# Running the compressed-KV projection of an MLA layer in half groups of 256 tokens, on 8 cores

## The chip, the cores and the metric

One Trainium2 chip, all 8 cores. Cores 0 to 3 take the first sequence of the batch, cores 4 to 7 the second. There is no exchange between cores. The metric is device microseconds of the slowest core for one execution of the whole program.

## The reference

One layer: `x + attention(LN(x)) + ffn(LN(x))` for x of 2 x 4096 x 4096. The part that matters here is the key/value side of the attention:

```python
xn = _layernorm(x, axis=-1)
ckv = hidden_states @ Wkv_a                       # 4096 -> 512 + 64
compressed, k_pe = (ckv[..., :KV_RANK], ckv[..., KV_RANK:])
kv = _rmsnorm(compressed, kv_a_ln_w) @ Wkv_b
...
k_pe = _apply_rope(k_pe, cos, sin)
```

The rest is the query side (rank 1536), causal softmax attention with 32 heads, the output projection, and a feed-forward part with a dense base matrix and 28 rank-8 adapters of which two are taken per token.

## The kernel before, in words

Each core computes the keys and values of its whole sequence (4096 tokens) and the queries of 8 tiles of 128 tokens. The program has four stages with barriers between them: stage 0 (LayerNorm of all tokens, transposition, `Wkv_a`, RMS norm, rope of the key part), stage 1 (the same for the own tiles with `Wq_a`), stage 2 (attention, head pair by head pair), stage 3 (output projection and feed-forward). The instructions of each engine are written in program order by a small helper, `Prog.do`, whose line 64 is the line that the profile names for all of them, so the rows are told apart by their tile names. Semaphores `p`, `v`, `a` count TensorE, VectorE and ScalarE; DMAs have rings of four (SyncE) and eight (GpSimd) semaphores.

Stage 0 is a loop over 8 groups `g` of 4 tiles of 128 tokens. For a tile `t`:

- GpSimd's queue loads `x_full` to `p0_x[t % 2]` with a cast to bf16, once the LayerNorm two tiles before has read the buffer.
- VectorE runs eight `bn_stats` (tile name `p_bn`), an aggregation and small operations, with two activations on ScalarE, and writes the normalised tile to `p0_xn[t % 2]`. It starts only when the transpose of tile `t - 2` has landed, because that reads the same buffer.
- SyncE issues one DMA transpose of 128 x 4096 from `p0_xn[t % 2]` into the columns of the tile in `p0_xnTg`, the transposed group (32 blocks of 128 features by 512 tokens). The first of a group also waits for the matmuls of the group before (`xnT_war`).

After the four tiles TensorE multiplies. For each of five chunks `mc` of the 576 output features (four of 128, one of 64) it runs 32 matmuls of 512 moving columns into one of three PSUM banks `ps_ck`; here a round is one such chunk. After each of the first four rounds VectorE copies the bank to `p0_cf`, squares it into the single buffer `p0_sq`, and TensorE adds the squares over the features by a matmul with a column of ones into `ps_ss`:

```python
ck_evac[mc % 3] = mark("v")
wait("tensor", "v", ck_evac[mc % 3])
...
do("tensor", "matmul", ps_ss[0:1, :], g_ones_col[:], sqs,
   start=(mc == 0), stop=(mc == 3), inc="p")
```

The next round stands behind that matmul on TensorE. The square of a chunk waits for the ones-column matmul of the chunk before. The tail of a group follows: the fifth chunk is copied (`p_kpef`), the mean of squares is taken (`p_ssr`), two activations give its inverse root, a matmul spreads it over the partitions (`ps_bc`), VectorE scales the four chunks into `g_cnorm`, and a rotation matmul and three operations of VectorE make the rope part `g_kpe`. On VectorE the next group's first LayerNorm stands behind all this in the queue.

Of the kernel before, what the change touches and what calls it, by code (L numbers as in the profile page):

```python
# [7 lines left out]
BF16 = mybir.dt.bfloat16  # L8
# [29 lines left out]
class Prog:  # L38
# [15 lines left out]
    def do(self, eng, meth, *args, inc=None, **kw):  # L54
        sem = amt = None
        r = None
        if inc is not None:
            key, amt = inc if isinstance(inc, tuple) else (inc, 1)
            self.cnt[key] += amt
            sem = self.sems[key]  # L60
            r = self.cnt[key]

        def f(e, meth=meth, args=args, kw=kw, sem=sem, amt=amt):
            ins = getattr(e, meth)(*args, **kw)  # L64
            if sem is not None:
                ins.then_inc(sem, amt)

        self.q[eng].append(f)
        return r
# [9 lines left out]
    def wait(self, eng, key, val):  # L79
        if val <= 0:  # L80
            return
        self.q[eng].append(lambda e, s=self.sems[key], v=val: e.wait_ge(s, v))
# [9 lines left out]
    def mark(self, key):  # L92
        return self.cnt[key]
# [9 lines left out]
def build_nc(debug=0, p0_groups=8, do_p0c=True, p0_stage=100, npairs=NPAIR):  # L103
# [58 lines left out]
    with es_root:  # L162
        P = Prog(nc, es_root)
        do, wait, mark = P.do, P.wait, P.mark

        def sb(name, shape, dt, stack):
            return stack.enter_context(nc.sbuf_tensor(name, shape, dt))

        def ps(name, stack, shape=None):
            return stack.enter_context(  # L170
                nc.psum_tensor(name, shape or [128, 512], F32))
# [11 lines left out]
        tok_con = [P.dma("gpsimd", dst[:], src) for dst, src in  # L183
                   [(g_ident, ident_in), (g_qlnw, qlnw), (g_kvlnw, kvlnw)]]
        do("gpsimd", "memset", g_ones_col[:], 1.0, inc="q")
        do("gpsimd", "memset", g_ones_row[:], 1.0, inc="q")
        c_consts_q = mark("q")

        es0 = ExitStack()
        with es0:  # L190
            x_sb = [sb(f"p0_x{i}", [128, D], BF16, es0) for i in range(2)]
            xn_sb = [sb(f"p0_xn{i}", [128, D], BF16, es0) for i in range(2)]
            xnT_g = sb("p0_xnTg", [128, 32 * 512], BF16, es0)
            wkva_sb = sb("p0_wkva", [128, 32 * 576], BF16, es0)

            rk_sb = sb("p0_rk", [64, 64], BF16, es0)
# [13 lines left out]
            rsr = sb("p0_rsr", [1, 512], F32, es0)  # L210
            rbc = sb("p0_rbc", [128, 512], F32, es0)

            ps_ck = [ps(f"ps_ck{i}", es0) for i in range(3)]
            ps_ss = ps("ps_ss", es0)
            ps_bc = ps("ps_bc", es0)
            ps_rk = ps("ps_rk", es0)
# [1 line left out]
            tok_p0 = [  # L218
                P.dma("gpsimd",
                      wkva_sb[:].rearrange("p (k f) -> p k f", k=32),  # L220
                      wkv_a.rearrange("(k p) f -> p k f", p=128)),
                P.dma("gpsimd", rk_sb[:], rk_in),
            ]
# [30 lines left out]
                return mark("v")  # L254

            tr_marks = [None, None]
            ck_evac = [0, 0, 0]
            xnT_war = 0
            prev_rope_v = 0
            prev_ssr_v = 0  # L260
            prev_kpe_a = 0
            prev_prk = 0
            for g in range(p0_groups):
                for tt in range(4):
                    t = g * 4 + tt
                    par = t % 2
                    if t >= 2:
                        wait("gpsimd", "v", ln_state[par])
                    gl = P.dma("gpsimd", x_sb[par][:],
                               x_full[t * 128:(t + 1) * 128, :])  # L270
                    P.wait_t("vector", gl)
                    P.wait_t("vector", tr_marks[par])
                    ln_state[par] = emit_ln(par)
                    if p0_stage < 2:
                        continue
                    wait("sync", "v", ln_state[par])
                    if tt == 0:
                        wait("sync", "p", xnT_war)
                    tr_marks[par] = P.dma(
                        "sync",  # L280
                        xnT_g[:].rearrange("p (k f) -> p k f", f=512)[:, :, tt * 128:(tt + 1) * 128],
                        xn_sb[par][:].rearrange("p (k f) -> p k f", f=128),
                        meth="dma_start_transpose")
                if p0_stage < 3:
                    continue
                P.wait_t("tensor", tr_marks[0])
                P.wait_t("tensor", tr_marks[1])
                if g == 0:
                    for tk in tok_p0 + tok_con:
                        P.wait_t("tensor", tk)  # L290
                    wait("tensor", "q", c_consts_q)
                wait("tensor", "a", prev_kpe_a)
                xnT3 = xnT_g[:].rearrange("p (k f) -> p k f", f=512)
                wk3 = wkva_sb[:].rearrange("p (k f) -> p k f", f=576)
                ssmm = [0, 0]
                first_ss = True
                for mc in range(5 if p0_stage >= 40 else 4):
                    pb = ps_ck[mc % 3]
                    wait("tensor", "v", ck_evac[mc % 3])
                    lo = mc * 128  # L300
                    hi = min(lo + 128, 576)
                    for kc in range(32):
                        do("tensor", "matmul",
                           pb[0:hi - lo, :], wk3[:, kc, lo:hi], xnT3[:, kc, :],
                           start=(kc == 0), stop=(kc == 31),
                           inc=("p" if kc == 31 else None))
                    pm = mark("p")
                    if mc < 4:
                        sqs = sq_f32[:]
                        wait("vector", "p", pm)  # L310
                        do("vector", "tensor_copy",
                           c_f32[:, mc * 512:(mc + 1) * 512], pb[:], inc="v")
                        cv = mark("v")
                        wait("vector", "v", cv)
                        wait("vector", "p", ssmm[0])
                        do("vector", "tensor_mul", sqs,
                           c_f32[:, mc * 512:(mc + 1) * 512],
                           c_f32[:, mc * 512:(mc + 1) * 512], inc="v")
                        ck_evac[mc % 3] = mark("v")
                        wait("tensor", "v", ck_evac[mc % 3])  # L320
                        if first_ss:
                            wait("tensor", "v", prev_ssr_v)
                            first_ss = False
                        do("tensor", "matmul", ps_ss[0:1, :], g_ones_col[:], sqs,
                           start=(mc == 0), stop=(mc == 3), inc="p")
                        ssmm[0] = mark("p")
                    else:
                        wait("vector", "p", pm)
                        do("vector", "tensor_copy", kpe_f[:], pb[0:64, :], inc="v")
                        kv_m = mark("v")  # L330
                        wait("scalar", "v", kv_m)
                        wait("scalar", "p", prev_prk)
                        do("scalar", "activation", kpe_bf[:], kpe_f[:], AF.Copy, inc="a")
                        ck_evac[mc % 3] = mark("v")
                kpe_vm, kpe_am = mark("v"), mark("a")
                pss = ssmm[0]
                if p0_stage < 4:
# [14 lines left out]
                   start=True, stop=True, inc="p")  # L352
# [11 lines left out]
                if p0_stage < 42:  # L364
# [5 lines left out]
                   start=True, stop=True, inc="p")  # L370
# [21 lines left out]
                prev_kpe_a = kpe_am  # L392
                if debug >= 1 and g == 7:
# [2 lines left out]
                    P.dma("gpsimd", dbg["d_misc"][:, 512:1024], kt1[:])  # L396
                    P.dma("gpsimd", dbg["d_misc"][:, 1024:1536], kt2[:])
                    P.dma("gpsimd", dbg["d_misc"][:, 1536:2048], cosf[:])
                xnT_war = mark("p")

            p0b_v, p0b_a = mark("v"), mark("a")

# [15 lines left out]
        with es1:  # L418
# [16 lines left out]
            tr_marks = [None, None]  # L435
            ln2 = {}
            for t in range(8):
# [7 lines left out]
                for i in range(8):  # L445
# [3 lines left out]
                       inc=("v" if i == 7 else None))  # L449
# [5 lines left out]
                   LN_EPS, inc="v")  # L455
# [39 lines left out]
            for mc in range(12):  # L495
# [10 lines left out]
                for half in range(2):  # L506
                    pb = ps_q[half]
                    wait("tensor", "v", qevac[half])
                    for kc in range(32):
                        do("tensor", "matmul", pb[:],  # L510
                           wq3[par][:, kc, :], xo3[:, kc, half * 512:(half + 1) * 512],
                           start=(kc == 0), stop=(kc == 31),
                           inc=("p" if kc == 31 else None))
                    pm = mark("p")
# [13 lines left out]
                       start=(mc == 0), stop=(mc == 11), inc="p")  # L528
# [17 lines left out]
               start=True, stop=True)  # L546
            do("tensor", "matmul", ps_qb[1][:], g_ones_row[:], qrsr[0:1, 512:1024],
               start=True, stop=True, inc="p")
# [17 lines left out]
        if debug != 1:  # L566
# [30 lines left out]
            for dst, src in [(cosq_sb, cosq), (sinq_sb, sinq),  # L597
                             (masks_sb, masks), (rq_sb, rq_in)]:
                tk = P.dma("gpsimd", dst[:], src)
# [126 lines left out]
            if True:  # L726
# [89 lines left out]
                for p in range(npairs):  # L816
                    for stp in range(NSLOT):
                        for h01 in ((0, 1) if p % 2 == 0 else (1, 0)):
# [4 lines left out]
                                p=p, h01=h01, s=s, stp=stp, nk5=nk5,  # L823
# [36 lines left out]
        else:  # L860
# [34 lines left out]
            for kc in range(32):  # L895
# [4 lines left out]
                for tch in range(8):  # L900
                    do("tensor", "matmul", ps_l[:, tch * 28:(tch + 1) * 28],
                       xk[par][:, tch * 128:(tch + 1) * 128], gw3[:, kc, :],
                       start=(kc == 0 and tch == 0), stop=(kc == 31),
                       skip_group_check=True)
                for er in range(2):
                    for half in range(2):
# [3 lines left out]
                           start=(kc == 0), stop=(kc == 31),  # L910
                           skip_group_check=True,
                           inc=("p" if (er == 1 and half == 1) else None))
# [6 lines left out]
            for tch in range(8):  # L919
                lo = lg_sb[:, tch * 28:(tch + 1) * 28]  # L920
# [33 lines left out]
                   inc="p")  # L954
# [14 lines left out]
            for er in range(2):  # L969
                for half in range(2):  # L970
                    if er == 1:
# [4 lines left out]
                       start=True, stop=True, inc="p")  # L976
# [44 lines left out]
            for dc in range(8):  # L1021
# [7 lines left out]
                for kc in range(32):  # L1029
# [8 lines left out]
                    for qc in range(8):  # L1038
                        if kc == 0:
# [3 lines left out]
                           start=(kc == 0), stop=False)  # L1043
# [160 lines left out]
```

How the kernel before makes its waits and increments, by code:

```python
        def f(e, meth=meth, args=args, kw=kw, sem=sem, amt=amt):  # L63
            ins = getattr(e, meth)(*args, **kw)
            if sem is not None:
                ins.then_inc(sem, amt)
# [12 lines left out]
    def wait(self, eng, key, val):  # L79
        if val <= 0:
            return
        self.q[eng].append(lambda e, s=self.sems[key], v=val: e.wait_ge(s, v))
```

## Time and profile before

| | us |
|---|---|
| median of 2 timed runs | 6434.42 (6394.51 and 6474.34) |
| profiled execution, its own time | 6153.71 |
| its span, slowest core | 6151.8 |
| stage 0, to the end of the last group | 0 to about 1199 |
| stage 1 | about 1199 to 1650 |
| stage 2 | about 1650 to 4820 |
| stage 3 | about 4820 to 6152 |

Busy time over the span: TensorE 3819.0 us (62%), VectorE 1887.9 (31%), ScalarE 1696.6 (28%), GpSimd 444.9 (7%). The chain of waits that ended last is 54% TensorE and 20% DMA; the DMA transposes of stage 0 alone are 7% of the span in it. A page of the profile gives for each group of instructions the busy time, the mean duration and the idle time ahead of it with the releaser; the rows behind this section come from such views.

### The profile page before, as it was taken

To read this page: it belongs to the slowest core of one execution; us is meant where nothing else is said; L and a number is where in the kernel's file an instruction comes from. 1 tells how busy PE (TensorE), PEld (TensorE's weight loads), DVE (VectorE), ACT (ScalarE), POOL (GpSimd) and SP (SyncE) were. 2 spreads that over 40 slices of the span, in tenths; PEclk is the share of its full clock that TensorE was granted. 3 is DMA by queue.
4 is the path that set the end of the run, shared out by engine and by line. 5 is a ranking of instruction groups with operands and counts; after the bars stand their busy time and mean duration, and the time that the engine had idled before them with its cause. 6 is when DMAs were issued, how large, how long until landed. Compare 5 with 4: busy or idle time off the path is not lost.

```text
span 6151.8 us, 55137 instructions; the slowest of 8 cores (6115.0 to 6151.8 us)
## 1 busy us (share of the span) xinstructions
PE 3819.0 (62%) x17980; PEld 1749.3 (28%) x17980; DVE 1887.9 (31%) x2827; ACT 1696.6 (28%) x1812; POOL 444.9 (7%) x773
## 2 busy tenths in 40 slices
PE   0233332208567776777667777677777538888887
PEld 0111111103233333333233333333333213333333
DVE  1222223321244444444444444444444010000000
ACT  0000000000054455544565455554555100000000
POOL 0000000000000000000000000000000112222222
PEclk9667666659877766777667776777767569999998
DMA  9755555595333323333243332333232465555555
GB/s 101 56 57 57 56 57 57 68 149 52 53 58 58 60 52 69 61 61 61 48 74 60 62 60 52 69 60 61 53 64 57 86 159 89 89 89 89 87 86 93
DMA packets 960482, 434.94 MB, mean 71 GB/s; under 512 B 832978, under 2 KB 935392, under 8 KB 954608
## 3 DMA queue, kind: packets, MB, share of 16 engines
q0 software_dynamic: 197072, 238.45, 23.3%
q1 hardware_dynamic: 763136, 192.98, 21.8%
q8 instruction: 155, 2.54, 0.2%
q14 instruction: 119, 0.97, 0.1%
HBM read 362.92 MB, written 34.08 MB: 65 GB/s over the span
## 4 chain that ended last, share of the span: by engine, by line
PE 54%; DMA 20%; issue 8%; DVE 8%; ACT 7%; SPq 2%; another core or an unknown queue 0%; POOL 0%; DVEq 0%; ACTq 0%; POOLq 0%
PE ps_b L64 30%; PE ps_acc L64 15%; DMA p_xnTg<-p_xn 7%; DMA p_pt<-p_pb 6%; PE ps_ck L64 5%; ACT p_pb L64 5%; PE ps_q L64 3%; DVE p_bn L64 2%; SPq L64 2%; DMA p_xnTown<-p_xn 2%; ACT p_sco L64 1%; DMA p_bw<-base_wt 1%; DMA out<-p_os 1%; DMA p_xk<-xnT_scr 1%; DVE p_sco L64 1%
## 5 line engine op out<-in xcount | busy, mean ns | idle before, releaser
L64 PE MATMUL ps_b<-p_pt,p_vp 128*128 128x128 bf16 x4608 | 489.8, 295 | 563.4 <-DMA p_pt<-p_pb 426.0
L64 PE MATMUL ps_ck<-p_xnTg,p_wkva 128*128 128x512 bf16 (+1 forms) x1280 | 302.4, 397 | 763.1 <-DMA p_xnTg<-p_xn 763.1
L64 PE MATMUL ps_b<-p_kn,p_qn 128*128 128x512 bf16 x1152 | 615.4, 534 | 239.0 <-ACT p_sco L64 220.2
L64 ACT ACTIVATE p_pb<-p_pb,p_zr 128x4096 bf16<-128x4096 bf16 (+7 forms) x256 | 567.0, 2215 | 694.4 <-DVE p_zr L64 693.7
L64 DVE TENSOR_REDUCE p_nm<-p_sco 128x1 f32<-128x4096 f32 (+7 forms) x256 | 653.6, 2553 | 76.5 <-DVE p_sco L64 40.0
L64 ACT ACTIVATE p_sco<-ps_b 128x512 f32<-128x512 f32 x896 | 521.3, 593 | 469.8 <-PE ps_b L64 463.6
L64 PE MATMUL ps_acc<-p_wt,p_of 128*128 128x512 bf16 x2048 | 496.7, 386 | 244.1 <-DMA p_bw<-base_wt 244.1
L64 PEld LDWEIGHTS ps_b<-p_pt,p_vp 128*128 128x128 bf16 x4608 | 435.1, 137 | 655.2 <-issue 655.0
L64 PE MATMUL ps_b<-g_kpe,p_qpe 64*128 64x512 bf16 x1152 | 609.2, 529 | 0.0
L64 ACT ACTIVATE p_pb<-p_sco,p_nm 128x4096 bf16<-128x4096 f32 (+7 forms) x256 | 564.6, 2206 | 96.0 <-DVE p_o L64 90.6
L64 DVE SCALAR_TENSOR_TENSOR p_sco<-ps_b,p_masks 128x512 f32<-128x512 f32 x256 | 176.5, 690 | 1133.2 <-PE ps_b L64 1074.7
L64 PE MATMUL ps_acc<-p_bw,p_xf 128*128 128x512 bf16 x2048 | 488.5, 382 | 0.0
L64 PEld LDWEIGHTS ps_ck<-p_xnTg,p_wkva 128*128 128x128 bf16 (+1 forms) x1280 | 129.9, 104 | 946.6 <-issue 818.9
L64 DVE TENSOR_TENSOR p_os<-ps_acc,p_xs 128x512 f32<-128x512 f32 x64 | 43.0, 690 | 1138.1 <-PE ps_acc L64 1068.7
L64 PEld LDWEIGHTS ps_acc<-p_wt,p_of 128*128 128x128 bf16 x2048 | 202.9, 99 | 495.8 <-issue 261.4
L64 DVE BATCH_NORM_STATS2 p_bn<-p_x 128x6 f32<-128x512 bf16 x320 | 193.6, 679 | 402.8 <-DMA p_xnTg<-p_xn 276.6
L64 PEld LDWEIGHTS ps_b<-p_kn,p_qn 128*128 128x128 bf16 x1152 | 125.8, 109 | 586.7 <-issue 586.6
L64 PE MATMUL ps_q<-p_xnTown,p_wqa 128*128 128x512 bf16 x768 | 172.3, 383 | 190.5 <-DMA p_wqa<-wq_a 190.5
L64 PE MATMUL ps_b<-g_qnorm,p_wqb 128*128 128x512 bf16 x1152 | 255.5, 383 | 47.1 <-DMA p_wqb<-wq_b 47.1
L64 PEld LDWEIGHTS ps_acc<-p_bw,p_xf 128*128 128x128 bf16 x2048 | 201.9, 99 | 247.2 <-issue 10.1
L64 PE MATMUL ps_b<-p_wkvb,g_cnorm 128*128 128x256 bf16 x2048 | 245.6, 284 | 38.1 <-DVE p_vp L64 19.6
L64 PEld LDWEIGHTS ps_b<-g_kpe,p_qpe 64*128 64x128 bf16 x1152 | 113.3, 98 | 440.9 <-issue 440.9
(115 smaller groups left out, 2391.5 us busy)
## 6 DMA issues: line engine op xcount, KB each, us to landing
p_x<-x_full POOLq DMA_DIRECT2D x32, 1024.0 KB, 23.2
p_wt<-wo POOLq DMA_DIRECT2D x256, 128.0 KB, 3.8
p_bw<-base_wt POOLq DMA_DIRECT2D x256, 128.0 KB, 4.0
p_wqb<-wq_b POOLq DMA_DIRECT2D x16, 1152.0 KB, 10.5
p_xs<-x_own POOLq DMA_DIRECT2D x8, 2048.0 KB, 9.5
out<-p_os POOLq DMA_DIRECT2D x64, 256.0 KB, 2.4
p_wqa<-wq_a POOLq DMA_DIRECT2D x12, 1024.0 KB, 9.8
p_x<-x_own POOLq DMA_DIRECT2D x8, 1024.0 KB, 18.7
```

Source lines behind the costliest of these rows:

```text
L64: ins = getattr(e, meth)(*args, **kw)
```

## The change

The group of 512 tokens is transposed into two buffers of 256 tokens each, `p0_xnTh[0]` and `p0_xnTh[1]`, which together have the size of the one before. After the second tile of a group TensorE multiplies these 256 tokens with all five chunks (the even half), and after the fourth tile the other 256 (the odd half). Both halves of a chunk share a PSUM bank: the even half writes columns 0 to 255, the odd half columns 256 to 511 without a start flag. There are five `ps_ck` banks in place of three, so that all chunks stay open; with `ps_ss`, `ps_bc` and `ps_rk` these are all eight. The copies, squares and ones-column matmuls come behind the odd half, and each copy waits for its own chunk's mark.

```diff
-            xnT_g = sb("p0_xnTg", [128, 32 * 512], BF16, es0)
+            xnT_h = [sb(f"p0_xnTh{i}", [128, 32 * 256], BF16, es0)
+                     for i in range(2)]
...
-            ps_ck = [ps(f"ps_ck{i}", es0) for i in range(3)]
+            ps_ck = [ps(f"ps_ck{i}", es0) for i in range(5)]
...
-                    if tt == 0:
-                        wait("sync", "p", xnT_war)
+                    hb = (t // 2) % 2
+                    if t % 2 == 0:
+                        wait("sync", "p", xnT_war[hb])
...
-                        xnT_g[:].rearrange("p (k f) -> p k f", f=512)[:, :, tt * 128:(tt + 1) * 128],
+                        xnT_h[hb][:].rearrange("p (k f) -> p k f", f=256)[:, :, (t % 2) * 128:(t % 2) * 128 + 128],
...
+                    if t % 2 == 1:
+                        hg_odd = (tt == 3)
+                        P.wait_t("tensor", tr_marks[0])
+                        P.wait_t("tensor", tr_marks[1])
...
+                        if not hg_odd:
+                            wait("tensor", "a", prev_kpe_a)
...
+                        col = slice(0, 256) if not hg_odd else slice(256, 512)
...
+                        for mc in range(5 if p0_stage >= 40 else 4):
+                            pb = ps_ck[mc]
+                            if not hg_odd:
+                                wait("tensor", "v", ck_evac[mc])
+                            lo = mc * 128
+                            hi = min(lo + 128, 576)
+                            for kc in range(32):
+                                do("tensor", "matmul",
+                                   pb[0:hi - lo, col], wk3[:, kc, lo:hi],
+                                   xnT3[:, kc, :],
+                                   start=(kc == 0 and not hg_odd),
+                                   stop=(kc == 31),
+                                   skip_group_check=True,
+                                   inc=("p" if kc == 31 else None))
+                            if hg_odd:
+                                odd_marks.append(mark("p"))
+                        xnT_war[hb] = mark("p")
...
                 for mc in range(5 if p0_stage >= 40 else 4):
-                    pb = ps_ck[mc % 3]
-                    wait("tensor", "v", ck_evac[mc % 3])
...
-                    pm = mark("p")
+                    pb = ps_ck[mc]
+                    pm = odd_marks[mc]
```

TensorE, first group of stage 0, before (`ps_ck` is a chunk of the projection, `ps_ss` the sum of squares, `ps_bc` and `ps_rk` belong to the tail):

```order
L64 MATMUL ps_ck<-p_xnTg,p_wkva 128x512 x32
L64 MATMUL ps_ss<-p_sq,g_ones_col 1x512
L64 MATMUL ps_ck<-p_xnTg,p_wkva 128x512 x32
L64 MATMUL ps_ss<-p_sq,g_ones_col 1x512
L64 MATMUL ps_ck<-p_xnTg,p_wkva 128x512 x32
L64 MATMUL ps_ss<-p_sq,g_ones_col 1x512
L64 MATMUL ps_ck<-p_xnTg,p_wkva 128x512 x32
L64 MATMUL ps_ss<-p_sq,g_ones_col 1x512
L64 MATMUL ps_ck<-p_xnTg,p_wkva 64x512 x32
L64 MATMUL ps_bc<-p_rsr,g_ones_row 128x512
L64 MATMUL ps_rk<-p_kpebf,p_rk 64x512
```

The same group on TensorE, now:

```order
L64 MATMUL ps_ck<-p_xnTh,p_wkva 128x256 x128
L64 MATMUL ps_ck<-p_xnTh,p_wkva 64x256 x32
L64 MATMUL ps_ck<-p_xnTh,p_wkva 128x256 x128
L64 MATMUL ps_ck<-p_xnTh,p_wkva 64x256 x32
L64 MATMUL ps_ss<-p_sq,g_ones_col 1x512 x4
L64 MATMUL ps_bc<-p_rsr,g_ones_row 128x512
L64 MATMUL ps_rk<-p_kpebf,p_rk 64x512
```

The 160 matmuls of 512 columns have become twice 160 of 256 columns, and the four ones-column matmuls have moved from between the chunks to behind all of them.

VectorE's row has not moved. The end of the first group is shown, from the last chunk's copy to the next group's first `bn_stats` (`p_sq` is the square, `p_ssr` the mean of squares):

```order
L64 COPY p_cf<-ps_ck 128x512
L64 TENSOR_TENSOR p_sq<-p_cf 128x512
L64 COPY p_kpef<-ps_ck 64x512
L64 TENSOR_SCALAR p_ssr<-ps_ss 1x512
L64 COPY p_rbc<-ps_bc 128x512
L64 SCALAR_TENSOR_TENSOR g_cnorm<-p_cf,g_kvlnw,p_rbc 128x512 x4
L64 TENSOR_TENSOR p_kt<-p_kpef,p_cosf 64x512
L64 TENSOR_TENSOR p_kt<-ps_rk,p_sinf 64x512
L64 TENSOR_TENSOR g_kpe<-p_kt 64x512
L64 BN_STATS p_bn<-p_x 128x6 x8
```

The pair of copy and square stands there four times, as before, and the next group's LayerNorm still follows the whole tail.

## Rows read from the trace of the kernel before

**Rows 1.** The page's first line: span and the spread over cores.

```profile
span 6151.8 us, 55137 instructions; the slowest of 8 cores (6115.0 to 6151.8 us)
```

**Rows 2.** Stretches, core 5: us, busy PE PEld DVE ACT POOL, PEclk, DMA share, GB/s.

```profile
199.00:301.00 102.00, 0.00 (x0) 0.01 (x1) 27.30 (x49) 1.62 (x8) 3.23 (x6) 0.50 1.07 85
301.00:360.00 59.00, 43.48 (x171) 17.15 (x171) 12.14 (x19) 1.79 (x3) 0.00 (x0) 0.90 0.00 1
506.00:586.00 80.00, 0.00 (x0) 0.00 (x0) 27.09 (x49) 1.62 (x8) 3.24 (x6) 0.50 0.98 108
...
926.00:1013.00 87.00, 0.00 (x0) 0.00 (x0) 27.34 (x49) 1.62 (x8) 3.23 (x6) 0.50 1.01 100
```

**Rows 3.** Waits of TensorE, first 1,200 us: total us, times, longest.

```profile
PE ps_ck L64 <- DMA p_xnTg<-p_xn: 763.1, 8, 140.6
```

**Rows 4.** Chain of waits, group 1: start us, us, what.

```profile
199.39 4.84 DVE p_bn L64 x8
...
207.17 45.78 DMA p_xnTg<-p_xn
...
278.93 21.74 DMA p_xnTg<-p_xn
...
301.02 9.87 PE ps_ck L64 x32
...
313.75 7.03 PE ps_ck L64 x32
...
359.90 4.84 DVE p_bn L64 x8
```

**Rows 5.** The same chain, group 3.

```profile
506.17 4.84 DVE p_bn L64 x8
...
558.79 15.13 SPq L64
...
574.07 12.43 DMA p_xnTg<-p_xn
...
586.84 8.63 PE ps_ck L64 x32
...
645.43 4.84 DVE p_bn L64 x8
```

**Rows 6.** V projection in stage 2: timeline of TensorE, and one stretch.

```profile
1925.76 4.42 PE L64 MATMUL ps_b<-p_wkvb,g_cnorm 128*128 128x256 bf16 x39
...
1932.00:1934.00 2.00, 2.00 (x21) 1.80 (x19) 1.94 (x6) 0.00 (x0) 0.00 (x0) 1.00 1.28 291
```

**Rows 7.** Group 1's first round: a weight load, and one microsecond's stretch.

```profile
302.25 0.15 PEld L64 LDWEIGHTS ps_ck<-p_xnTg,p_wkva 128*128 128x128 bf16 x1 [0.28 <-issue]
...
302.00:303.00 1.00, 1.00 (x4) 0.29 (x2) 0.00 (x0) 0.00 (x0) 0.00 (x0) 0.50 0.00 0
```

**Rows 8.** Timeline of group 1: a square, its ones-column matmul, the mean of squares.

```profile
321.73 0.69 DVE L64 TENSOR_TENSOR p_sq<-p_cf 128x512 f32<-128x512 f32 x1 [0.17 <-DVE p_cf L64]
...
322.57 1.02 PE L64 MATMUL ps_ss<-p_sq,g_ones_col 128*1 128x512 f32 x2 [1.81 <-DVE p_sq L64]
...
351.01 0.67 DVE L64 TENSOR_SCALAR p_ssr<-ps_ss 1x512 f32<-1x512 f32 x1
```

**Rows 9.** First pair of transposes of group 3, by tile: issue, landing.

```profile
L64 SPq DMA_TRANSPOSE p_xnTg<-p_xn x2: 18452/19135/19818, 514.0 to 533.9; - x2
...
DMA to landing us min/median/max: 20.5/28.7/37.0
```

**Rows 10.** The last group: its first pair by tile, its last transpose in the chain.

```profile
L64 SPq DMA_TRANSPOSE p_xnTg<-p_xn x2: 19466/20137/20808, 1079.5 to 1099.1; - x2
...
DMA to landing us min/median/max: 22.8/30.9/38.9
...
1133.85 5.55 DMA p_xnTg<-p_xn
```

**Rows 11.** The attention's 256 transposes, by tile `p_pt`.

```profile
DMA to landing us min/median/max: 2.4/4.9/10.5
```

More of the change, by code:

```diff
@@ L256, in build_nc @@
             tr_marks = [None, None]
-            ck_evac = [0, 0, 0]
-            xnT_war = 0
+            ck_evac = [0, 0, 0, 0, 0]
+            xnT_war = [0, 0]
             prev_rope_v = 0
@@ L262, in build_nc @@
             prev_prk = 0
+            odd_marks = []
             for g in range(p0_groups):
@@ L282, in build_nc @@
                         xn_sb[par][:].rearrange("p (k f) -> p k f", f=128),
                         meth="dma_start_transpose")
+                    if t % 2 == 1:
+                        hg_odd = (tt == 3)
+                        P.wait_t("tensor", tr_marks[0])
+                        P.wait_t("tensor", tr_marks[1])
+                        if t == 1:
+                            for tk in tok_p0 + tok_con:
+                                P.wait_t("tensor", tk)
+                            wait("tensor", "q", c_consts_q)
+                        if not hg_odd:
+                            wait("tensor", "a", prev_kpe_a)
+                        xnT3 = xnT_h[hb][:].rearrange("p (k f) -> p k f", f=256)
+                        wk3 = wkva_sb[:].rearrange("p (k f) -> p k f", f=576)
+                        col = slice(0, 256) if not hg_odd else slice(256, 512)
+                        if hg_odd:
+                            odd_marks.clear()
+                        for mc in range(5 if p0_stage >= 40 else 4):
[12 more added lines that the diff above has]
+                                   inc=("p" if kc == 31 else None))
+                            if hg_odd:
+                                odd_marks.append(mark("p"))
+                        xnT_war[hb] = mark("p")
@@ L284, in build_nc @@
                 if p0_stage < 3:
                     continue
[L286 to L294, printed above, removed]
@@ L297, in build_nc @@
                 for mc in range(5 if p0_stage >= 40 else 4):
-                    pb = ps_ck[mc % 3]
-                    wait("tensor", "v", ck_evac[mc % 3])
[L300 to L306, printed above, removed]
-                    pm = mark("p")
+                    pb = ps_ck[mc]
+                    pm = odd_marks[mc]
                     if mc < 4:
@@ L318, in build_nc @@
                            c_f32[:, mc * 512:(mc + 1) * 512], inc="v")
-                        ck_evac[mc % 3] = mark("v")
-                        wait("tensor", "v", ck_evac[mc % 3])
+                        ck_evac[mc] = mark("v")
+                        wait("tensor", "v", ck_evac[mc])
                         if first_ss:
@@ L333, in build_nc @@
                         do("scalar", "activation", kpe_bf[:], kpe_f[:], AF.Copy, inc="a")
-                        ck_evac[mc % 3] = mark("v")
+                        ck_evac[mc] = mark("v")
                 kpe_vm, kpe_am = mark("v"), mark("a")
@@ L398, in build_nc @@
                     P.dma("gpsimd", dbg["d_misc"][:, 1536:2048], cosf[:])
-                xnT_war = mark("p")
             p0b_v, p0b_a = mark("v"), mark("a")
```

## The prediction

> **What bounds the kernel now.** I read the spans of the cores first. The eight stand within 0.6% of each other, so a change that every core makes alike moves the slowest one by as much [rows 1]. The profiled execution took 6153.71 us around a span of 6151.8 us; the two timed runs took 6394.51 and 6474.34 us, some 280 us more, and no view says where. I work the change out against the profiled execution and subtract it from both levels.
>
> Next, the first 1,200 us in alternating stretches [rows 2]. TensorE and the DMA engines take turns. From 199 to 301 us the matmuls are at 0.00 and the DMA share is 1.07; from 301 to 360 us the matmuls are busy and the DMA share is 0.00. Eight such pairs, one per group of four tiles, make the stage. The waits put it in one row: TensorE waits 763.1 us for the transposes, in 8 waits [rows 3]. The chain of waits shows how a group is strung together [rows 4]. In group 1, two LayerNorms start on VectorE at 199.39; their transposes go out from 207.17; the first lands 45.78 us later, at 252.95, and only then has the third tile's LayerNorm a buffer to write; the second pair of transposes has landed at 300.67 (278.93 + 21.74); then five rounds of 32 matmuls, each followed by a ones-column matmul that waits for VectorE's copy and square; then a tail, and the next group's LayerNorm at 359.90. So from the last landing to the next LayerNorm about 59 us pass in which no DMA moves. These 59 us are what the change works on. The transposes and loads before them bound the stage, and stay.
>
> **What the change moves.** The orders show that only TensorE's row is reordered; VectorE, ScalarE, GpSimd and SyncE keep theirs. SyncE gets one more wait per group, at the third tile, for the matmuls of the previous group's second half. These ended before VectorE could start the LayerNorm that the same transpose needs, so it is over when it is reached: 0 us, and behind it in SyncE's queue only transposes. TensorE's even half waits for transposes 0 and 1, for the kpe copy on ScalarE and for the evacuations of the previous group; all but the transposes lie before this group's first LayerNorm on VectorE. Queued behind it on TensorE is only the odd half, which needs later transposes anyway.
>
> **Step 1, what goes.** In group 1 from the first matmul, 301.02, to the next LayerNorm, 359.90: 58.9 us. It consists of the first round at 9.87 us, four rounds of about 7.05, four gaps of 2.8 between the end of a round and the next one, and 9.5 of tail [rows 4]. Group 3 has 586.84 to 645.43, 58.6 us [rows 5].
>
> **Step 2, the odd half.** 160 matmuls with 256 moving columns stand where 160 with 512 stood. The trace has this shape in the V projection of the attention: 39 in 4.42 us at a granted clock of 1.00 (2.4 GHz), 113 ns each [rows 6]. 160 x 0.113 = 18.1 us. The burst follows an idle stretch, and the clock then stands at 0.50 (1.2 GHz) [rows 7]. In the first round that costs 9.87 - 7.03 = 2.8 us, and it is time lost and not matmuls, so the same for narrower ones. 20.9 us. Bounds: half the columns in half the time, 38.2 / 2 = 19.1, below; all of it at 1.2 GHz, above: weight loads there follow each other at 0.15 + 0.28 = 0.43 us for 512 columns [rows 7], so 160 x 0.213 = 34.1. I take 20.9, since in the chain the second round already takes 7.03 us, which is 2.4 GHz [rows 4].
>
> The Trainium skill, "TensorE: Matmul & The Clock Gate", section "Back-to-back issue gap", gives sustained spacings of 131 ns for 512 columns and 81 for 128. Between these, an estimate by that page is 98 ns for 256, which would make the odd half some 2.4 us shorter per group and the gain about 19 us larger in all. The trace has 221 ns for 512 columns (7.05 / 32) and 113 for 256, so here the rows decide against the page.
>
> **Step 3, the squares.** The four ones-column matmuls now stand behind all 160. VectorE copies and squares the first chunk during the burst, copies the second and then stops, because the square has one buffer and the second square waits for the first ones-column matmul. After the burst's end the chain is four of these (1.02 us each) with three squares (0.69) between them and about 0.3 us of hand-over per step [rows 8]: 4.1 + 2.1 + 0.9 = 7.1 us. The copies of the third and fourth chunk and of kpe lie beside it. Before, these gaps were 11.2 us, so part of the gain is theirs. Bounds: with two buffers' worth of overlap 4.1; without any overlap 4 x 2.8 = 11.2.
>
> **Step 4, the tail** from the mean of squares on VectorE, 351.01, to 359.90 is unchanged: 8.9 us [rows 4, 8].
>
> **Step 5, the even half** costs the same 20.9 us, beside the second pair of transposes. In group 3 the first pair's second transpose goes out at 533.9 and lands 20.5 us later, at 554.4 [rows 9]; the burst then ends at 575.3, while the second pair lands at 586.5 (574.07 + 12.43) [rows 5]: 11 us to spare. The tightest is the last group, which has no more loads: second transpose of the first pair at 1121.9, burst to 1142.8, odd half free from 1139.4 [rows 9, 10]. It starts 3.4 us late, but with the clock up, which gives back 2.8. If the cover were gone altogether, 20.9 us per group would come back and the gain with it.
>
> **Sum.** After the last landing: 20.9 + 7.1 + 8.9 = 36.9 us where 58.6 to 58.9 stood; 21.9 us per group, 175 us in eight. One term has no row: DMA stretches of the same content take 80.7 us (group 3, 506.17 to 586.84) and 101.6 us (group 1, 199.39 to 301.02) [rows 4, 5], so they bend to something outside this core's order, and shorter pauses between them could bring more of these collisions. Its bounds are 0 and the difference of these two, 21 us per group; I take 1.3 per group, 10 us, near the lower end because the stretches of groups 3 and 6 are 81 and 87 us and group 1's stands alone [rows 2]. Forecast: 165 us less. The profiled execution would be 5989 us, and the median of the runs 6434.4 - 165 = 6269.4 us. I give the second as the predicted time, since it is the runs that are timed; own range of the forecast 6240 to 6300.
>
> **Rivals.** C, transposes lose while the even half runs. For: before, not one matmul of this stage ran beside a transpose [rows 2]. In the attention, where they do, a transpose can take 10.5 us to land (maximum), against 5.55 for the last one here, without loads or matmuls beside it [rows 10, 11], a factor 1.89. If during the 20.9 us of the burst the DMA goes at 1/1.89, it loses 9.8 us per group, 79 in all: 175 - 79 = 96 us less, 6338 us. Against: in the V projection the matmuls are busy 2.00 of 2.00 us, and the queues beside them move 291 GB/s [rows 6] against 85 to 108 here [rows 2].
>
> D, the slower one. The whole second pair of transposes and loads, 27.7 us in group 3 (558.79 to 586.5), is slowed by 1.89: 24.7 us per group, 197 in all, against 175 gained: 22 us more, 6456 us. The place is SyncE's third and fourth transpose; it decides from a factor 1.79 on (21.9 / 27.7 = 0.79), and makes 2% slower from 2.4. The same rows speak against it, and the largest landing of the attention holds only for its widest tiles.
>
> The Trainium skill, "SBUF — State Buffer", section "SBUF: two separate sides", says that engine ports and DMA ports are disjoint and cannot slow each other. By that rule C and D would be nothing; the 291 GB/s beside full matmuls agree with it, and the large landings of the attention may have other loads beside them.
>
> B, the clock stays down. With two short bursts per group the odd half and the squares run at 1.2 GHz: 34.1 - 20.9 = 13.2 us, plus four ones-column matmuls of twice 1.02 us [rows 8], 4.1 us. Gain 21.9 - 17.3 = 4.6 per group, 37 us, 6397 us. Against: before, the clock is up within the first 10 us of a burst [rows 4], and this one lasts 20.
>
> **How the numbers follow.** Forecast 0.65, C 0.18, B 0.08, D 0.06, something unseen 0.03. 2% of 6434.42 is 129 us, about what a measurement tells from no change. Faster by more: 0.63 of the forecast's, 0.05 of C's, 0.01 unseen: 0.69. Within 2%: the rest of the forecast, 0.02, of C, 0.13, B, 0.08, and half of D, 0.03: 0.26. Slower: half of D and unseen, 0.05. The range goes up to C, 6338, with a little for the runs' own scatter: 6345; it leaves B and D out. Downwards it takes in the profiled execution's level with the whole 175 gained and 10 more: 5970.
>
> **What would show it.** Right: TensorE's bursts of 160 in about 21 us, twice per group; the DMA share 0.9 and more beside the even half; next LayerNorm 37 us after the odd half's start; 8 periods that are 21 to 22 us shorter; the stages behind unchanged. Wrong: an even burst that ends after the second pair's landing; the second pair beyond 40 us (C, D); a granted clock of 0.50 through the odd half (B); ones-column matmuls more than 2 us apart. If the periods shrink as said and the total does not, a later stage gives it back.

## The result and the profile after

The changed kernel takes 0.9787 of the time before (95% interval 0.975 to 0.9825), which is 2.1% less. The median of its 12 runs is 6092.26 us, against 6390.59 us for 10 runs of the kernel before. In part of the executions of either kernel the cores of a die show a lower granted clock and take some per cent longer; the ratio and the times given for the variants below leave those executions out, the two timed runs shown at first are as long as these (280 us above the profiled execution), and the parts of stage 0 for e1 and e13 below come from such an execution. The fastest of these runs are 6024.18 and 6157.51 us.

The page's first line of the changed kernel:

```profile
span 6022.3 us, 57718 instructions; the slowest of 8 cores (5940.9 to 6022.3 us)
```

The slowest core is 129.5 us shorter than in [rows 1]. Core by core the gain is 125 to 185 us, on the mean 152. Nearly all of it lies in stage 0: its last group ends at 1186 us before and at 1042 us now, mean of the eight cores, 144 us less.

Waits of TensorE in the first 1,200 us, changed kernel, which answer to [rows 3] (total us, times, longest):

```profile
PE ps_ck L64 <- DMA p_xnTh<-p_xn: 645.1, 15, 103.4
PE ps_ss L64 <- DVE p_sq L64: 23.0, 24, 1.3
```

There are 15 waits for transposes in place of 8, and less in total. It should be 16; in the last group the odd half finds its data there already. The waits for squares have fallen from 58.5 us to 23.0, and from 32 to 24: the first square of each group is ready before its ones-column matmul is reached.

The chain of waits in group 1 of the changed kernel, core 5, which answers to [rows 4] (start us, us, what):

```profile
176.39 4.84 DVE p_bn L64 x8
...
225.63 4.86 DVE p_bn L64 x8
...
233.43 20.96 SPq L64
...
254.54 16.84 DMA p_xnTh<-p_xn
...
271.52 20.41 PE ps_ck L64 x160
...
293.83 1.03 PE ps_ss L64 x2
...
295.79 1.03 PE ps_ss L64 x2
...
298.88 0.69 DVE p_ssr L64
...
308.74 4.84 DVE p_bn L64 x8
```

The row SPq is the time in which SyncE is busy issuing a transpose. From the odd half's first matmul to the next LayerNorm it is 37.2 us, where [rows 4] had 58.9. The odd half is one block of 160 matmuls of 20.41 us. The ones-column matmuls stand 1.96 us apart, and the mean of squares starts 7.0 us after the burst. The even half is not in the chain at all. Where it is, the stretches of that group show (us, busy time of PE, PEld, DVE, ACT, POOL, then granted clock, DMA share, GB/s):

```profile
229.00:249.00 20.00, 19.32 (x160) 16.61 (x160) 10.09 (x19) 0.81 (x4) 1.11 (x2) 0.91 0.82 89
249.00:271.00 22.00, 0.00 (x0) 0.00 (x0) 0.00 (x0) 0.00 (x0) 0.00 (x0) 0.59 1.25 112
271.00:308.00 37.00, 27.02 (x171) 18.28 (x171) 11.23 (x17) 1.89 (x3) 0.00 (x0) 0.82 0.00 0
```

The burst of 160 ends in 19.32 us beside a DMA share of 0.82, and 22 us before the second pair has landed. The last row is the pause: the DMA share is still 0.00 there, as in [rows 2], but the pause is 37 us and no longer 59.

What went another way than forecast does not stand out on one core. I took every group 1 to 6 on all 8 cores, 48 in each kernel, from the timelines of VectorE and TensorE. In each, three parts: S1 from the group's first LayerNorm to the third tile's LayerNorm; S2 from there to the odd half's first matmul, which is the last landing; and the pause from there to the next LayerNorm. Means, and in brackets the standard error:

| us | S1 | S2 | S1 + S2 | pause |
|---|---|---|---|---|
| before | 46.6 (0.5) | 38.3 (0.5) | 84.8 (0.7) | 58.8 |
| changed | 46.1 (0.3) | 44.6 (0.4) | 90.7 (0.5) | 36.9 |

The pause came out as worked out. The DMA stretch, which was to stay, has grown by 5.9 us, all of it in S2. That is the question for the experiments.

### The profile page after: what moved, and what is told of

It reads as the page before. It is cut to its first block, busy times and chain, and to the rows that moved or that the text cites. A ratio compares the mean times of both kernels' runs of the same rounds, so it can differ in the third digit from the quotient of the medians.

```text
span 6022.3 us, 57718 instructions; the slowest of 8 cores (5940.9 to 6022.3 us)
## 1 busy us (share of the span) xinstructions
PE 3854.3 (64%) x19260; PEld 1892.1 (31%) x19260; DVE 1886.5 (31%) x2827; ACT 1698.1 (28%) x1812; POOL 445.0 (7%) x773
## 4 chain that ended last, share of the span: by engine, by line
PE 53%; DMA 21%; issue 8%; DVE 7%; ACT 7%; SPq 3%; POOL 0%; DVEq 0%; ACTq 0%; POOLq 0%
PE ps_b L64 30%; PE ps_acc L64 15%; DMA p_xnTh<-p_xn 7%; DMA p_pt<-p_pb 6%; ACT p_pb L64 5%; SPq L64 3%; PE ps_ck L64 3%; PE ps_q L64 3%; DMA p_xnTown<-p_xn 2%; DVE p_bn L64 2%; ACT p_sco L64 1%; DMA p_bw<-base_wt 1%; DMA p_xk<-xnT_scr 1%; DMA out<-p_os 1%; DMA p_xf<-xnT_scr 1%
## 5 line engine op out<-in xcount | busy, mean ns | idle before, releaser
L64 PE MATMUL ps_ck<-p_xnTh,p_wkva 128*128 128x256 bf16 (+1 forms) x2560 | 314.4, 289 | 645.1 <-DMA p_xnTh<-p_xn 645.1
L64 PEld LDWEIGHTS ps_ck<-p_xnTh,p_wkva 128*128 128x128 bf16 (+1 forms) x2560 | 268.6, 106 | 692.3 <-issue 653.7
## 6 DMA issues: line engine op xcount, KB each, us to landing
p_wt<-wo POOLq DMA_DIRECT2D x256, 128.0 KB, 3.1
p_bw<-base_wt POOLq DMA_DIRECT2D x256, 128.0 KB, 3.3
```

## The experiments

Stage 0 is measured in all of them by the same parts, from one profiled execution each. The transposes and loads are the same in number and size in every one.

**e1: are the matmuls beside the DMAs to blame?** In the even half only the first and last matmul of each chunk stay:

```diff
-                            for kc in range(32):
+                            for kc in (range(32) if hg_odd else (0, 31)):
                                 do("tensor", "matmul",
```

> Left out: of the even half's 32 matmuls per chunk only the first and the last are kept, so some 10 short matmuls stand beside the second pair of transposes in place of 160; everything else is the changed kernel. Measure: the DMA stretch, from the next group's first LayerNorm to the last landing, mean over groups 1 to 6 and 8 cores (before 84.8 us, changed kernel 90.7 us), and the pause after it (58.8 and 36.9 us). Theory 1, matmuls beside transposes and loads slow them: stretch back to 85, pause 37. Theory 2, shorter pauses make the DMA stretches of different cores coincide more and they share something: stretch stays at 91. Theory 3, the transposes are slower because their destination has blocks of 256 columns in place of 512: stays at 91.

S1 45.7, S2 44.4, pause 37.3 us. The even half is practically gone and S2 has not moved (44.2 us on cores 0 to 3, 44.6 on cores 4 to 7): theory 1 falls. (The variant leaves out most of the even half's sums, so only stage 0 is read from it.)

**e2: is it the short pause?** All matmuls behind the fourth tile:

```diff
-                    if t % 2 == 1:
-                        hg_odd = (tt == 3)
+                    for hg_odd in ((False, True) if tt == 3 else ()):
+                        hb = 1 if hg_odd else 0
```

> The changed kernel with the even half's matmuls moved behind the fourth tile, directly ahead of the odd half: nothing of TensorE beside the DMAs, long pause of about 320 x 0.113 + 2.8 + 7.1 + 8.9 = 55 us. Theory 1 and theory 2: stretch back to 85. Theory 3 (destination blocks): stretch stays at 91.

S1 45.9, S2 44.3, pause 54.7 us. With the pause nearly as long as before and nothing beside the DMAs, S2 is still 44.3. Theories 1 and 2 both had 85 for S1 + S2; it is 90.2.

**e3: the same question from the other side**, the kernel before with a short pause:

```diff
-                    for kc in range(32):
+                    for kc in range(16, 32):
```

> The kernel before with 16 of the 32 matmuls of each chunk left out: no TensorE work beside the DMAs, destination blocks as before, but a pause of about 40 us. Theory 1 and theory 3: stretch at 85 as before. Theory 2 (coinciding stretches): about 90.

S1 46.6, S2 38.0, pause 41.5 us (it leaves out half of every sum, and only stage 0 is read). Shortening the pause alone adds nothing. So the growth belongs to something in the text of the changed kernel, and my candidate was the destination's layout.

**e7: is it the layout?** One tensor with blocks of 512 columns, everything else as changed:

```diff
-            xnT_h = [sb(f"p0_xnTh{i}", [128, 32 * 256], BF16, es0)
-                     for i in range(2)]
+            xnT_g = sb("p0_xnTg", [128, 32 * 512], BF16, es0)
+            xnT_v = xnT_g[:].rearrange("p (k f) -> p k f", f=512)
...
-                                   xnT3[:, kc, :],
+                                   xnT_v[:, kc, hb * 256:hb * 256 + 256],
```

> The changed kernel with one thing undone: the two halves lie again in one tensor of 32 blocks of 512 columns, as before the change; TensorE's halves read columns 0 to 255 and 256 to 511 of each block. Same order on every engine. The two runs before showed the DMA stretch at 90 us with the two tensors whether or not matmuls stand beside it, and 84.6 with the one tensor and a short pause; all of the 6 us lie between tile 3's LayerNorm and the last landing (before 38.3 us, changed kernel 44.6 us). Theory 3a, the layout of the destination does it: that part 38.3, stretch 84.8, pause 37, period 122, 35 to 45 us less than the changed kernel. Theory 3b, something else that all these variants share (five PSUM banks, the added wait in SyncE's queue, the copies that follow in another order): that part stays at 44.6, period 128.

S1 45.9, S2 44.6, pause 37.0 us; ratio to the kernel before 0.9793 (0.9703 to 0.9883), as for the changed kernel. The third theory falls as well, and my expectation with it. Two further variants of the layout went at the same time. e8, blocks 288 columns apart:

```diff
-            xnT_h = [sb(f"p0_xnTh{i}", [128, 32 * 256], BF16, es0)
+            xnT_h = [sb(f"p0_xnTh{i}", [128, 32 * 288], BF16, es0)
```

> The changed kernel with two tensors whose blocks stand 288 columns (576 bytes) apart instead of 256 (512 bytes). If the distance of 512 bytes itself, a power of two, is the cause: the part from tile 3's LayerNorm to the last landing goes to 38.3 us. If it is that second pairs go to a tensor of their own and not between the columns of the first pair: it stays at 44.6.

S1 46.8, S2 44.8. And e9, the two tensors exchanged:

```diff
-                    hb = (t // 2) % 2
+                    hb = 1 - (t // 2) % 2
```

> The changed kernel with the two tensors exchanged: first pairs go to the second tensor, second pairs to the first. If the address of the second tensor is slow: the 6 us move to the first pair (46.1 to 52, second part 44.6 to 38). If block distance or the pair's place in the group decides: nothing changes (46.1 and 44.6).

S1 46.1, S2 45.2. Neither block distance, nor sharing of a block, nor address.

**e11: what is left.** The kernels with the long S2 (changed, e1, e2, e7, e8, e9) and those with the short one (before, e3) differ in five PSUM banks against three, the order of copies and matmuls during the pause, and one line on SyncE: the third transpose of a group waits for TensorE too. I had costed that line at 0 us, since the value is reached long before. It can be taken out safely: the third tile's LayerNorm stands on VectorE behind copies that waited for the same matmuls.

```diff
-                    if t % 2 == 0:
+                    if tt == 0:
                         wait("sync", "p", xnT_war[hb])
```

> The changed kernel without the wait for TensorE that it added to SyncE's queue ahead of the third transpose of a group (the LayerNorm that this transpose waits for anyway stands on VectorE behind copies that waited for the same matmuls, so the order stays safe). Layout, matmuls beside the DMAs, pause and address have been ruled out for the 6 us between tile 3's LayerNorm and the last landing (38.3 us before, 44.6 to 45.2 in all variants of the changed kernel). Theory W, the third wait, though long satisfied, makes the third transpose and what lies beside it slower: that part goes to 38.3 us, period 121 us, about 40 us less in all. Rival P, something else of these variants (five PSUM banks, copies and squares in another order): stays at 44.6.

S1 45.8 (0.4), S2 39.2 (0.5), pause 36.9 us. S2 is back, and only S2. Stage 0 ends at 1003 us, mean of the cores, 40 us earlier than in the changed kernel. The total was 5977.79 us, against 6024.18 for the fastest run of the changed kernel, 46 us less, and 6030.19 to 6051.09 for e7, e8 and e9; it is one value without an interval.

**e12: the line put into the kernel before.**

```diff
-                    if tt == 0:
+                    if tt in (0, 2):
                         wait("sync", "p", xnT_war)
```

> The kernel before with one more line: the third transpose of a group waits for TensorE too, for a value long reached. Theory W: the part from tile 3's LayerNorm to the last landing goes from 38.3 to about 44.6 us, the period from 143.6 to about 150. Rival P: 38.3 and 143.6 as before.

S1 46.3 (0.5), S2 44.4 (0.6): from 38.3, 6.1 us more, from one wait for a value long reached. The period is 151.0 us. Its pause was 60.4 us, 62.0 on cores 4 to 7 and 58.8 on cores 0 to 3; on the latter, whose pause is that of the kernel before, S2 is 45.2 against 38.6 before. Its total, 6266.38 us, is one value, some 100 us above the kernel before, of which stage 0 explains 46. Both directions agree in S2; rival P falls.

In the chain of waits this looks as follows, the third transpose being the SPq row and S2 running from the LayerNorm above it to the matmuls below. Changed kernel, group 3, core 5:

```profile
486.04 4.85 DVE p_bn L64 x8
...
493.83 19.40 SPq L64
...
530.49 20.63 PE ps_ck L64 x160
```

Without the third wait (e11), group 4, core 5:

```profile
570.62 4.86 DVE p_bn L64 x8
...
578.38 15.50 SPq L64
...
609.45 20.28 PE ps_ck L64 x160
```

The kernel before with the third wait (e12), group 2, core 5:

```profile
400.57 4.86 DVE p_bn L64 x8
...
408.38 19.51 SPq L64
...
440.68 10.13 PE ps_ck L64 x32
```

SyncE issues the third transpose 7.79 and 7.81 us after the LayerNorm's start with the wait, and 7.76 us without: the wait holds nothing up to speak of. What grows is the time that SyncE is busy issuing the transpose (SPq), 19.40 and 19.51 us against 15.50, and in [rows 5] 15.13. The single values scatter by several us (27.46 in group 4 of the changed kernel). The means over 48 groups are 22.5 us (changed) and 21.1 (e12) with the wait, 15.5 (e11) and 14.8 (before) without.

The DMA packets show the same. Packets of the transposes in the 16 us that begin 12 us after the third tile's LayerNorm, first in the kernel before, group 3, then in e12, group 2, core 5 (number, MB, share of 16 engines):

```profile
q1 hardware_dynamic: 1578, 0.40, 70.9%
...
q1 hardware_dynamic: 835, 0.21, 64.6%
```

On the mean of 8 cores and five groups (1 to 6 without 5, which the last section comes to), these 16 us have 1,068 packets of transposes in the kernel before and 1,097 in e11, but 621 in e12 and 724 in the changed kernel. The loads move about 1.6 MB in all four. So with the wait the transposes fall behind, and the loads gain nothing by it.

**e13: does the first transpose pay the same?** It has had such a wait in the kernel before too. Both waits out:

```diff
-                    if t % 2 == 0:
-                        wait("sync", "p", xnT_war[hb])
```

> The changed kernel without either wait for TensorE in SyncE's queue: the first transpose of a group loses its wait too (it is implied in the same way: its LayerNorm stands on VectorE behind copies that waited for all these matmuls). If a satisfied wait ahead of a transpose costs in itself: the first pair's part falls like the second's did, 46 to about 40 us, stretch 79, period 116, another 45 us less than without the third wait (5977.79 us). If it is particular to the second pair: the parts stay at 46 and 39, period 122, equal to the version without the third wait.

S1 41.3 (0.8), S2 39.3 (0.3), together 80.6 us, pause 38.1; S1 is 41.5 us on cores 0 to 3 and 41.1 on cores 4 to 7. The first pair gives back 4.5 us. The kernel before has the same wait at its first transpose and may carry the same cost; there it was not tried. From group 1's start to group 7's it is 712 us, mean of the cores, against 731 in e11. At the end of stage 0 9 us of this are left, 994 against 1003, since group 0 took longer. The total does not show it: 6011.85 us, one value, where 5977.79 stood without the third wait alone. The 45 us that I had expected did not come, and whether the total keeps these 4.5 us per group stays open for this kernel.

**e6: a version that takes the pause away.** The pause of 37 us exists because the next LayerNorm stands behind the tail on VectorE. Here the next group's first two tiles come first:

```diff
+            tile_in(0)
+            tile_in(1)
             for g in range(p0_groups):
-                for tt in range(4):
+                for tt in (1, 3):
...
+                    if tt == 3:
+                        tile_in(t - 1)
+                        tile_in(t)
...
+                if g + 1 < p0_groups:
+                    tile_in(g * 4 + 4)
+                    tile_in(g * 4 + 5)
```

`tile_in` holds the load, LayerNorm and transpose of a tile, unchanged; the last two calls stand between the odd half and the copies.

> The changed kernel with the LayerNorms and transposes of the next group's first two tiles moved ahead of this group's copies and squares in VectorE's, SyncE's and GpSimd's order. If, as the profile has it, the pause of 37 us exists only because the next LayerNorm stands behind the tail on VectorE, DMA goes on through it and the period of a group falls from 128 to about 90 us (LayerNorm of tile 3 at 37 + 8 us after the last landing, then 40 us for the second pair): about 250 to 290 us less than the changed kernel in all. If the DMA work alone needs more (rival: 14 us per tile and its share of x loads, collisions over the whole period), the period stays at 100 to 110 us: 130 to 190 us less.

5765.38 and 5785.25 us, some 250 us less than the changed kernel. The period of a group, from one kpe activation to the next, mean of 8 cores and 5 groups, is 90.4 us; in the changed kernel it is 128.0 by the same measure. e10, with the one tensor in it:

> The version with the next two tiles' LayerNorms first, and the one tensor of 512-column blocks. If the layout is the cause of the longer transposes, its gain adds: about 6 us per group, 40 us less than the version with two tensors (5785 us profiled). If not: equal.

5755.22 to 5772.26 us, period 91.5, ratio to before 0.9343 (0.926 to 0.9426). No gain by the layout here either. And e14, with two tensors again and SyncE's waits for TensorE handed to VectorE:

```diff
                 P.wait_t("vector", tr_marks[par])
+                if t % 2 == 0:
+                    wait("vector", "p", xnT_war[(t // 2) % 2])
                 ln_state[par] = emit_ln(par)
...
-                if t % 2 == 0:
-                    wait("sync", "p", xnT_war[hb])
```

> The version with the next two tiles first (5765 to 5785 us), with SyncE's waits for TensorE taken over by VectorE ahead of the LayerNorm, so that SyncE's transposes wait for VectorE alone. Its periods were about 90 us, made of two pairs of transposes with a LayerNorm ahead of each. If the satisfied waits cost 6 us at each of two places: 12 us per group less, about 5690 us. If only at the second pair: about 5730. If the waits cost only beside a late load, which this order has everywhere: no change, 5765 to 5785.

5708.63 to 5720.84 us, ratio to before 0.9244 (0.9184 to 0.9304). The period is 82.7 us, 7.7 less than with the waits on SyncE; here the gain shows in the total, about 60 us. It lies between the two sizes that I had expected, 12 us per group and 6. The same dependency costs 7.7 us per group less on VectorE than on SyncE. Two stretches of 100 us of this version, core 5, columns as above:

```profile
300.00:400.00 100.00, 63.00 (x455) 48.53 (x456) 53.38 (x93) 4.32 (x15) 4.34 (x8) 0.77 0.96 110
400.00:500.00 100.00, 57.73 (x381) 39.96 (x378) 44.52 (x76) 5.39 (x14) 3.23 (x6) 0.77 1.10 104
```

The matmuls and the DMAs no longer take turns: TensorE is busy 58 and 63% of them, and the DMA share is 0.96 and 1.10.

## Why the prediction was right, and where a term was off

The sign, the mechanism and the size to within a quarter were right: forecast 165 us less, measured 129.5 on the slowest core of the profiled execution and 152 on the mean core. By 2.1% the change lies just beyond the 2% that I had taken as the bound, and the interval reaches across it, 1.75% to 2.5%: the kernel is faster, but whether by more than 2% is not settled.

Step 1, what goes: 58.6 to 58.9 us, mean of the eight cores 58.8. Right.

Step 2, the odd half: 20.9 us forecast, 20.41 in group 1 above, 19.23 to 20.63 in the others. The pace of 113 ns holds, and the clock rises within the burst. In the Trainium skill's page "TensorE: Matmul & The Clock Gate", section "Back-to-back issue gap", the spacing for 256 columns would lie near 98 ns (an estimate between its two figures). The trace does not agree: it has (20.41 - 2.8) / 160 = 110 ns.

Step 3, the squares: 7.1 us forecast; from the burst's end at 291.93 to the mean of squares at 298.88 it is 7.0. Right. The copies of later chunks are hidden as expected.

Step 4, the tail: 8.9 us forecast, 298.88 to 308.74 is 9.9. The granted clock is 0.99 from 298 to 301 us and 0.50 from 301 to 304, so behind the chain of short matmuls it has fallen before the matmul that spreads the inverse root:

```profile
301.15 2.04 PE L64 MATMUL ps_bc<-p_rsr,g_ones_row 1*128 1x512 f32 x2 [2.37 <-ACT p_rsr L64]
```

In group 1 before, the same pair took 1.09 us. In sum 36.9 forecast and 36.9 measured on the mean of 48 groups: a little less in step 2 and a little more here. That the sum agrees to a tenth is in part luck, since the two errors cancel.

Step 5, the even half under cover: right, with 22 us to spare in group 1. In the last group it ends 1 us after the landing, and 320 matmuls run in one piece:

```profile
1007.78 36.94 PE ps_ck L64 x320
```

Its whole cost is thus 36.94 us where two bursts would be 40; this is the clock kept up, as worked out.

**The term that was mis-sized** is the one that I had called "One term has no row", 1.3 us per group between bounds of 0 and 21. It measured 5.9 us, for six groups 35 us in place of 8. Its size was left low and its cause was wrong: I named "something outside this core's order" and collisions that shorter pauses would bring. A shorter pause alone adds nothing (e3), nor do the matmuls beside the DMAs (e1, e2); what adds it is the wait that the change puts on SyncE. The part on what the change moves said of it: "it is over when it is reached: 0 us". It was over, and it cost 6 us (e11, e12). With it in its place the sum is 8 x 21.9 - 6 x 5.9 = 140 us, and stage 0 ended 144 us earlier.

The rivals: C, with 9.8 us lost per group to matmuls beside the transposes, is wrong in mechanism, though the second pair did grow by 6.3 us; without e1 and e2 it would have been believed. D did not come; from the third transpose's issue, 7.8 us after the LayerNorm's start, the second pair grew by a factor of (44.6 - 7.8) / (38.3 - 7.8) = 1.21, far from the 1.79 that it needed. The Trainium skill's page "SBUF — State Buffer", section "SBUF: two separate sides", by which engine reads and DMA do not slow each other, holds here: S2 is 44.4 us without (e1) and 44.6 us with 160 matmuls beside it. Rival B, the clock down through the odd half, did not come.

That the median of all runs, 6092.26 us, stands below the forecast 6269.4 comes from the level: I had subtracted from the two runs at hand. It lies outside the range that I gave the forecast itself, 6240 to 6300, and inside the wide one, 5970 to 6345, which took in the level of the profiled execution. What the working gives is the difference of 165 us; the level was not worked out.

## What to carry to other kernels

A wait for a value long reached isn't free everywhere: ahead of a pair of DMA transposes on SyncE, with loads beside them, it cost 4.5 to 6 us per pair here. Where an earlier instruction in another queue implies it, or can carry it, leave it out there, and count waits on queues that issue transfers as a term of their own. And where an engine and the DMAs take turns, look at what stands in the queue between the end of one group and the start of the next: splitting the work hid 22 of its 59 us, for 2%, and reordering the queue took nearly the whole pause, for 6.6% (e10) and, with the waits moved, 7.6% (e14) against the kernel before.

## What the runs showed of the hardware that was not expected

One added wait, satisfied before it is reached, in front of the third transpose lengthens that transpose's issue and the landing of the pair by 6 us in 38, in two kernels and both directions. The transposes beside which no load runs are not touched: in the last group, which has none, S2 is 21.3 us with the wait (e12, e2) and 21.3 without (before). So it seems to need a load of 1 MB beside it, which GpSimd issues some 0.4 us later. The transpose goes out only 0.03 to 0.05 us later than without. How so small a thing sets the pace of the next 40 us was not found.

It is not that the wait changes which of the two transfers is ahead. With the wait the transpose's first packet stands before the load's in all 48 groups, at 8.98 us after the LayerNorm's start; without it (before, e11) in 40 of 48, at 8.93 us. In these 40, where the order is the same, the wait still costs 4.4 to 4.7 us: the pair lands at 38.8 us in the kernel before against 43.4 in e12, and at 39.8 in e11 against 44.2 in the changed kernel. The other eight are group 5 of every core. There, in the kernel before, e3 and e11, the transpose goes out 0.4 us later and behind the load, and the pair lands early, at 33.1 us in the kernel before against 46.5 in e12. So the mean of 6 us holds some 4.5 us in five groups and 10 to 13 in one. Why these three kernels have this delay in group 5, and the others not, is not known.

An added wait is also an added instruction in SyncE's queue. An instruction of another kind in its place was not tried, so whether it is the waiting or the place in time that counts is open.

The destination's layout made no difference to a DMA transpose: rows of 256 bytes at distances of 512, 576 and 1024 bytes, S2 of 44.6, 44.8 and 44.6 us.

In the last group, which has no loads, the matmuls of the even half do come with a later landing: the pair lands 22.5 us after its LayerNorm's start in the changed kernel and in e11, and 20.9 us in the kernels without 160 matmuls beside it (before, e1, e2). The transposes' data packets end at 20.4 us in either. On core 5 of the changed kernel the last two packets, of 4 bytes each, start behind a packet of 16 KB that the trace marks as instruction, at 21.3 us. So what came late there is not the transpose's data.
